# Last feed-forward: GpSimd applies a tile's normalization, and VectorE makes x's two scales by one-element operations

## The reference

```python
def _rmsnorm(x, g):  return g * (x * rsqrt(mean(x * x) + 1e-8))
def _act_quant(x):
    scale = 127.0 / clip(max(abs(x)), 1e-4, None)
    return clip(round(x * scale), -128, 127) / scale
def _ternary_quant(w):
    s = mean(abs(w)); return round(tanh(w / (s + 1e-8))) * arctanh(s)
def _linear_bit(x, w, g): return _act_quant(_rmsnorm(x, g)) @ _ternary_quant(w).T
h = silu(_linear_bit(x, w1, g1)) * _linear_bit(x, w2, g2)      # 512 -> 2048
x = _layernorm(x + _linear_bit(h, w3, g3))                      # 2048 -> 512
```

## Time and profile before

| what | value |
|---|---|
| median of 3 runs | 3251.03 us (3241.36 to 3251.85) |
| the profiled execution | 3245.8 us |
| its span, first to last instruction | 3244.0 us |
| granted TensorE clock over the span | 0.954 |
| last feed-forward, first to last instruction | about 2949.5 to 3238 us |
| busy in the span: PE, DVE, ACT, POOL | 87%, 65%, 55%, 44% |

### The profile page before, as it was taken

One profiled execution on the slowest core, in us unless ns is written; L12 is line 12 of the kernel. 1 busy time (PEld: TensorE's weight loads), 2 busy tenths in 40 slices (PEclk: granted clock), 3 DMA queues, 4 the chain that ended last, 5 costly groups with the idle time before them and its releaser, 6 DMA issues. The chain is left out here.

```text
span 3244.0 us, 64425 instructions
## 1 busy us (share of the span) xinstructions
PE 2827.4 (87%) x24738; PEld 2004.9 (62%) x24738; DVE 2104.0 (65%) x4863; ACT 1773.2 (55%) x3844; POOL 1431.7 (44%) x1539
## 2 busy tenths in 40 slices
PE   5999999967888887999999878989999999975786
PEld 3666666635666665777777656667666676652343
DVE  6677777667777776655555557766555555555896
ACT  4555555546878884333333267755444444454885
POOL 3444444435878884544454425551111112213563
PEclk8999999988989997999999989999999999987998
DMA  5000000010000012000000011002000110022000
GB/s 174 24 1 2 1 1 1 1 43 1 2 2 2 2 47 93 27 8 8 1 1 1 1 56 34 21 2 75 24 30 31 36 40 1 1 78 72 14 20 27
DMA packets 47124, 81.75 MB, mean 25 GB/s; under 512 B 5730, under 2 KB 15972, under 8 KB 46692
## 3 DMA queue, kind: packets, MB, share of 16 engines
q1 hardware_dynamic: 46820, 77.64, 7.2%
HBM read 73.44 MB, written 4.19 MB: 24 GB/s over the span
## 5 line engine op out<-in xcount | busy, mean ns | idle before, releaser
L1144 POOL TENSOR_TENSOR c_pT<-c_prob,c_pT 128x512 f16<-128x512 f32 x256 | 296.2, 1172 | 100.9 <-ACT c_pT L1094 98.5
L2027 POOL TENSOR_TENSOR c_prob<-c_prob,c_inv 128x512 f32<-128x512 f32 x128 | 133.1, 1042 | 302.1 <-DVE c_inv L2245 302.1
L789 DVE SCALAR_TENSOR_TENSOR a_pT<-psT,a_kvh_t,a_pT 128x256 f16<-128x256 f32 (+1 forms) x256 | 94.6, 411 | 169.0 <-ACT a_pT L695 169.0
L1421 DVE TENSOR_REDUCE c_peak<-psS 128x2 f32<-128x512 f32 x256 | 170.7, 684 | 36.6 <-PE psS L1247 34.0
L1144 POOL TENSOR_TENSOR a_pT<-a_prob,a_pT 128x384 f16<-128x384 f32 x128 | 120.8, 950 | 157.9 <-ACT a_pT L1094 157.2
L1337 ACT ACTIVATE c_prob<-psT 128x512 f32<-128x512 f32 x256 | 154.8, 605 | 62.2 <-PE psT L1266 41.6
L1094 ACT CAST c_pT<-c_prob 128x512 f16<-128x512 f32 x256 | 158.6, 620 | 0.0
L2161 ACT ACTIVATE c_prob<-c_prob,c_negmax 128x256 f32<-128x256 f32 x256 | 127.8, 501 | 55.2 <-DVE c_negmax L2237 54.2
L488 POOL TENSOR_TENSOR a_q_rot<-a_q_cos,a_q_sin 128x512 f32<-128x512 f32 x64 | 87.9, 1373 | 155.8 <-DVE a_q_sin L808 155.8
L507 POOL TENSOR_TENSOR a_prob<-a_prob,a_inv 128x128 f32<-128x128 f32 x128 | 52.4, 410 | 220.3 <-DVE a_inv L782 220.3
L1677 POOL TENSOR_TENSOR f_ch<-f_h,f_c 128x256 f32<-128x256 f32 x88 | 76.2, 866 | 142.6 <-DVE f_h L1894 142.4
(11 more groups left out here) (629 smaller groups left out, 11369.4 us busy)
## 6 DMA issues: line engine op xcount, KB each, us to landing
c_feed<-in_L_ffn_w1T SPq DMA_DIRECT2D x16, 512.0 KB, 3.6
c_feed<-in_L_ffn_w2T SPq DMA_DIRECT2D x16, 512.0 KB, 3.5
x_all<-in_x SPq DMA_DIRECT2D x8, 512.0 KB, 7.3
a_ring<-in_L_attn_WqT SPq DMA_DIRECT2D x8, 512.0 KB, 5.6
a_ring<-in_L_attn_WoutT SPq DMA_DIRECT2D x8, 512.0 KB, 4.2
a_feed<-in_L_xattn_Wq SPq DMA_DIRECT2D x8, 512.0 KB, 3.7
c_feed<-in_L_xattn_Wo SPq DMA_DIRECT2D x8, 512.0 KB, 4.0
c_feed<-in_L_ffn_w3T SPq DMA_DIRECT2D x8, 512.0 KB, 3.6
```

The lines of the kernel that those rows point to most:

```text
L789: last = dve.scalar_tensor_tensor(pT[1][:, r, m, m * P:N], T[:, m * N + m * P:(m + 1) * N], kvh_t[:, b % 2, m, H + h:H + h + 1], pT[0][:, ...
L1144: pool.tensor_tensor(pT[1][:, c % NPH, :], prob[:, c % NPX, :], pT[0][:, c % NPH, :], ALU.subtract)\
L1421: dve.tensor_reduce(peak[:, h, :], S, X_AXIS, ALU.max).then_inc(s.m_done, 1)
L2027: pool.tensor_tensor(prob[:, h % NPB, :, :], prob[:, h % NPB, :, :], inv[:, h % NPB, :].rearrange("p (n a) -> p n a", a=1).broadcast_to([P ...
```

## The change

The residual sum is written to `G.r` in SBUF and no longer back into the bank, and a new semaphore `y_read` says that the bank has been read. `down` waits for that. The statistics are taken from `G.r`. The last step, with its name `normal`, is moved from DVE to POOL, where it stands behind the root in the place of `rstd`. Since `G.r` holds two tiles, `measure` of tile t waits until `normal` of tile t - 2 is done. Apart from this, one DVE operation with two tensor inputs, which makes both numbers of `f_ax`, becomes two operations on one element each, whose factor is a per-row scalar.

```diff
@@ POOL
-                def rstd(t):
+                def normal(t):
                     if 0 <= t < T:
+                        n = t % 2
                         pool.wait_ge(s.var_ready, t + 1)
-                        pool.tensor_tensor(G.rstd[:, t % 2:t % 2 + 1], G.ve[:, t % 2:t % 2 + 1], G.minus_half[:, 0:1],
-                                           ALU.pow).then_inc(s.rstd_ready, 1)
+                        pool.tensor_tensor(G.rstd[:, n:n + 1], G.ve[:, n:n + 1], G.minus_half[:, 0:1], ALU.pow)\
+                            .then_inc(s.rstd_ready, 1)
+                        pool.wait_ge(s.rstd_ready, t + 1)
+                        pool.tensor_scalar(G.x[:, t, :], G.r[:, n, :], G.mv[:, n, 0:1], G.rstd[:, n:n + 1],
+                                           ALU.subtract, ALU.mult).then_inc(s.x_done, 1)
...
-                    rstd(t - 4)
+                    normal(t - 4)
@@ PE, down
                         if t:
-                            pe.wait_ge(s.x_done, t)
+                            pe.wait_ge(s.y_read, t)
@@ DVE, x_scale
-                        dve.tensor_tensor(ax[:, r, :], mx[:, r, :], c127[:, 0:2], ALU.mult).then_inc(s.qx_ready, 1)
+                        dve.tensor_scalar(ax[:, r, 0:1], mx[:, r, 0:1], c127[:, 0:1], None, ALU.mult)
+                        dve.tensor_scalar(ax[:, r, 1:2], mx[:, r, 1:2], c127[:, 1:2], None, ALU.mult)\
+                            .then_inc(s.qx_ready, 1)
@@ DVE, measure
                         dve.wait_ge(s.y_ready, t + 1)
-                        step(dve.scalar_tensor_tensor(Y[:, :], Y[:, :], hs[:, t % 4, 4:5], G.x[:, t, :], ALU.mult,
-                                                      ALU.add))
-                        step(dve.bn_stats(G.stats[:, n, :], Y[:, :]))
+                        if t >= 2:
+                            dve.wait_ge(s.x_done, t - 1)
+                        dve.scalar_tensor_tensor(G.r[:, n, :], Y[:, :], hs[:, t % 4, 4:5], G.x[:, t, :], ALU.mult,
+                                                 ALU.add).then_inc(s.y_read, 1)
+                        dve.wait_ge(s.y_read, t + 1)
+                        step(dve.bn_stats(G.stats[:, n, :], G.r[:, n, :]))
@@ DVE
-                def normal(t):
-                    if 0 <= t < T:
-                        n = t % 2
-                        dve.wait_ge(s.rstd_ready, t + 1)
-                        dve.tensor_scalar(G.x[:, t, :], Y[:, :], G.mv[:, n, 0:1], G.rstd[:, n:n + 1],
-                                          ALU.subtract, ALU.mult).then_inc(s.x_done, 1)
...
                     h_max(t - 1, 1)
-                    normal(t - 4)
```

More of the change, by code:

```diff
@@ L2334, in ffn1 @@
         s.rstd_ready, s.x_done, s.chain = sc.sem("rstd_ready"), sc.sem("x_done"), sc.sem("chain")
+        s.y_read = sc.sem("y_read")
         s.round_step = sc.sem("round_step")
```

## The result

In fast runs the changed kernel takes 1.0024 times the time of before, 95% interval 1.0015 to 1.0033: +7.8 us, from +4.9 to +10.7. The medians are 3256.30 us (20 runs, 3240.95 to 3261.08) and 3247.11 us before (20 runs, 3236.17 to 3252.76). It is slower: the change is small, but its whole interval lies above 1. The forecast was 3240 us and a gain of 10.

The account below looks back on a forecast made before the run. The prediction took a loop closed by both DVE and ACT, without slack, as the bound. Terms -1.7 - 7.7 - 8.2 - 0.8 + 12 T gave -10.2 us at T = 0.68, forecast 3240 us, range 3231 to 3250.

Parts of the forecast that it names:

- T: Time of the normalization moved to POOL, in no profile row; taken as 0.68 us, low end 0.62, high end 1.27.
- rival 1: Moved operation on POOL: two arithmetic stages priced like two inputs, T 1.04 to 1.6, time -5.9 to +0.8 us; chance 0.20.
- rival 2: Moved operation on POOL: two passes over the tile, 2.54 us, time +12.1 us, 3263; chance 0.06.
- 12 T - 18.4: Whole change in us: sum of early tiles, loop, end and last operation; -10.2 at T = 0.68.
- 13.5 + T: Tile period in the loop of the last stage, expected still 14.2 us.
- the double closing by DVE and ACT: Middle tiles: the 14.2 us loop is closed twice, by DVE and by ACT, with no slack in either.
- The first tiles should have given 1.7 us: Early tiles, from the short scales: 1.14 us in tile 0 and 0.58 in one more.
- T - 0.12: Tiles 5 to 15: how much later x_max starts behind POOL; less 0.58 for the scales, T - 0.70 a loop.
- my terms with T = 2.08 gave 7.5: End of the kernel: 8.2 us gained by freeing the bank earlier, and T - 0.76 added behind the last root.
- Rival 4: Last tiles: PE keeps its clock, down 14 and 15 stay at 3.62 us, 4.1 more gain, -14.3; chance 0.10.
- rival 3: Short scales still stand behind POOL: 8.1 us of gain missing, -2.1 us, 3249; chance 0.06.
- the middle of the stage gains nothing: Middle tiles: x_scale gives 0.58 us and weigh_x takes 0.56 back.

Follow-up runs that it names:

- The operations by themselves: Kernel before with 22 GpSimd operations added at its very start, each run alone with VectorE idle; 3281.52 us, one run.
- the move alone: Changed kernel with L2562 put back as one operation with two tensor inputs; ratio 1.0053 against before, +17.2 us.
- the operation twice: Changed kernel with the GpSimd normalization done twice, the first copy into an unread spare tile; ratio 1.012 against before, +39 us.
- the one product: Changed kernel with one product by a repeated factor replacing the two-stage operation, mean left out; ratio 0.9980 against before, -6.5 us.
- the operation at another place: Changed kernel with GpSimd's operation between the third and fourth product of h, one turn later, up to turn 16; ratio 0.9953 against before, -15.3 us.

## Why the prediction was wrong

**The step that failed is the price of the moved operation, T.** I took 0.68 us from a copy and a conversion, as "the nearest rows", and set 1.27 us, a product of two full tensors, as the high end. It takes 2.08. Both choices rested on counting inputs: one tensor in, so like a copy; certainly not above two tensors in. The operations by themselves show that the kind of operation sets the price. Neither rival 1 (its upper end was 1.6) nor rival 2 (two passes, 2.54) is the mechanism: one stage costs 1.52, and a second one 0.42 more. I had bounded an operation from above by another that merely seemed heavier, and the range went with it.

**The sum around it held.** 12 T - 18.4 at T = 2.08 is +6.6 us; the stage grew by 6.6, the span by 6.7, and the measured time by 7.8. The zero was said to be at T = 1.53. The period was said to be 13.5 + T: 15.58 at 2.08, 14.50 at 1.04, 17.64 at 4.15 where PE kept its clock. So the length of the operation explains the longer tile, and little is left in it for PE's lower clock: the slow transposes of some tiles. The loop, its lateness and the double closing by DVE and ACT were read rightly. What I had missed is the second loop through PE's `down`, only 0.3 us shorter; with POOL on the path it does not decide.

**That the total fits so well is in part luck.** The first tiles should have given 1.7 us. From `x_max` of tile 0 to that of tile 4 it is 73.9 us before and 73.4 after; I had read tile 3's gain as free, but the turn from tile 3 to 4 took 19.77 us where it took 18.87, with PE waiting 6.30 us before `up`. The turn to tile 5 cost 2.2 us where my terms give 2.0 (T - 0.12, since ACT had not waited for tile 4's scales), and the ten turns after it 14.2 where they give 13.8. Against these, the end from the last `x_max` to the last write is 45.3 us where it was 54.6, 9.3 less, and my terms with T = 2.08 gave 7.5. The difference is the last `down` at 3.63 us and not 6.04. But 6.04 is one execution's figure. In the other trace of the program before, that `down` took 5.31 us and the one before it 3.63, and the end 52.2: against that the end gives 6.9 us, and the whole stage (287.0) grows by 7.8. In the kernels with the move alone, the operation twice and the one product the stage lies 2 to 3 us beside the sum. Rival 4 had both last `down` at 3.62. Only tile 15's was, behind a wait of 1.45 us; tile 14's took 5.30, with 3.62 us of waiting ahead of its transposes.

**The scales.** 0.58 us on the operation was right, and L2568 never waits for POOL, so rival 3 fell. As part of this change, with POOL on the path, they are worth that (15.58 against 16.16). Alone they give 0.3, because of the second loop. I had said that "the middle of the stage gains nothing" from `normal` leaving DVE; where the operation does not stand on the path it gives the other 0.28, as the kernel with the operation at another place shows (13.60 against 13.88).

**What stays open.** In the first tiles PE's clock, its waits and the preparation of the weights act together, and no run here separates them: from `x_max` of tile 0 to that of tile 4 the traces range from 73.0 to 76.3 us. Why GpSimd's `tensor_scalar` takes 1.52 us where a copy takes 0.61, no run shows either. And when PE gets its full clock back after a wait can't be foretold from these traces. The kernel with the operation twice is 5 us above its stage by the ratio, within its interval of 29 to 49 us.

## What to carry to other kernels

An idle engine is not a free one: what counts is where in its stream the work lands. The same 2.08 us made the stage 22.5 us longer ahead of the product that the loop waits for than between the third and the fourth product of h, where GpSimd was idle. When the price of a moved operation is in no row, take no other operation's row as its upper bound; write the result as a function of the price, find the value at which the sign turns, and measure the operation before anything else. And do not take the stage of a single execution as exact: here the ends of the same program, in two executions, were 2.4 us apart.

## What the runs showed of the hardware

- GpSimd's two-stage operation with per-row factors takes 2.07 us for 128x512 in f32, and with one stage and a number 1.52; a product by a repeated factor takes 1.04, so two such operations would cost what the one fused operation does (2.08, an estimate from that row).
- A VectorE operation with two tensor inputs of two elements takes 0.91 us under a GpSimd product, and two one-element operations take 0.32 us from the start of the first to the end of the second.
- VectorE's SBUF to SBUF normalization takes 0.54 us alone and 2.18 in the median when GpSimd's `weigh_x` started 0.45 us before it.
- After waits of the same length PE ran at the full granted clock in one case and at half of it in another. The last two `down` of the kernel before, after 3.62 and 4.06 us of waiting, took 5.32 and 6.04 us in one trace (granted clock 0.68 and 0.59 over them) and 3.63 and 5.31 in another (1.00 and 0.68). Eight transposes took 1.03 us at 0.50 and 0.62 at 1.00, the first after 2.52 us of waiting in one place and 4.31 in another, the second after 2.80 and 3.37.
